# In a graph kernel's four narrow passes, gathers wait for the messages made from a ring's old rows, and the message writers wait for TensorE's sums

## The reference

```python
# first network, per layer
msg = h[src] * edge_weight[:, None]
h_neigh = segment_sum(msg, dst, num_segments=n) * inv_deg
h = h @ W_self[l].T + h_neigh @ W_neigh[l].T + b_neigh[l]
# second network, per layer
a = a_mu + jnp.exp(a_ls) * eps          # eps: one row of 64 for each edge
h = h * norm_out
m = h[src] * a
agg = segment_sum(m, dst, num_segments=n)
h = agg * norm_in @ W + b
```

## Time and profile before

| | |
|---|---|
| median of 3 runs | 11618.99 us (11612.03 to 11624.92) |
| the profiled execution | 11611.31 us, its span 11609.5 us |
| PE busy | 7401.4 us (64%) |
| DVE busy | 7264.5 us (63%) |
| POOL busy | 5339.7 us (46%) |
| ACT busy | 2333.6 us (20%) |
| gathers of the narrow passes (L526 from the node table) | 2496 of them, 2373.6 us busy, 1832.8 us idle ahead of them |

### The profile page before, as it was taken

The page is one execution under the profiler, slowest core; times in us unless marked ns, Lnnn a source line. Parts: engine busy times, 40 slices in busy tenths (PEclk is TensorE's granted clock), DMA queues, the critical chain, the costliest instruction groups (busy, mean ns, idle before and its releaser), DMA issues. The chain is left out here.

```text
span 11609.5 us, 162406 instructions
## 1 busy us (share of the span) xinstructions
PE 7401.4 (64%) x38309; PEld 5189.5 (45%) x38310; DVE 7264.5 (63%) x10358; ACT 2333.6 (20%) x8740; POOL 5339.7 (46%) x5631
## 2 busy tenths in 40 slices
PE   5887788677767765555558465654845555755557
PEld 4665566555555542333257233334732223623336
DVE  6665333455555555777799576778955556755558
ACT  1222444200000001111179111115910000000000
POOL 4555556455555534666400365650015554055650
PEclk8888888788878876777655666775567776966778
DMA  3333444344444436777569576764933333433333
GB/s 82 88 87 82 111 115 116 92 113 112 113 101 114 114 83 208 234 235 234 169 269 397 177 234 230 234 213 193 415 123 75 77 76 66 121 73 76 77 73 103
DMA packets 847434, 1713.98 MB, mean 148 GB/s; under 512 B 384448, under 2 KB 470131, under 8 KB 793063
## 3 DMA queue, kind: packets, MB, share of 16 engines
q1 hardware_dynamic: 462202, 1136.31, 28.3%
q0 software_dynamic: 206896, 411.57, 16.1%
q10 hardware_dynamic: 178256, 165.14, 4.2%
HBM read 1260.10 MB, written 452.33 MB: 148 GB/s over the span
## 5 line engine op out<-in xcount | busy, mean ns | idle before, releaser
L526 POOL DMA_INDIRECT gathered_rows<-node_table,index x2496 | 2373.6, 951 | 1832.8 <-issue 657.6
L691 PE MATMUL ps_G<-table_parts,low_onehots 125*128 125x320 bf16 x15600 | 2719.4, 337 | 278.6 <-issue 187.6
L546 PE MATMUL ps_sum<-messages,onehots 128*125 128x65 f32 (+3 forms) x13312 | 2110.0, 320 | 970.0 <-issue 629.7
L546 PEld LDWEIGHTS ps_sum<-messages,onehots 128*125 128x125 f32 x13312 | 2005.8, 235 | 1095.9 <-issue 1088.0
L526 POOL DMA_INDIRECT gathered_rows<-xl_table,index x1664 | 1572.5, 945 | 1972.1 <-issue 997.0
L526 POOL DMA_INDIRECT gathered_rows<-rel_table,index x1456 | 1383.9, 950 | 2113.6 <-ACT index L516 1177.7
L1507 PE MATMUL ps_Z<-xr,onehots_wide 125*128 x3328 | 1521.4, 616 | 1157.4 <-issue 638.9
L691 PEld LDWEIGHTS ps_G<-table_parts,low_onehots 125*128 125x128 bf16 x15600 | 1677.0, 110 | 1174.2 <-issue 270.3
L721 DVE TENSOR_TENSOR rows_by_feature<-ps_G,fifth_onehots 128x320 f32<-128x320 f32 x1040 | 507.3, 488 | 2475.9 <-remote 1853.1
L1507 PEld LDWEIGHTS ps_Z<-xr,onehots_wide 125*128 125x128 f32 x3328 | 809.3, 260 | 1869.1 <-issue 1776.8
L1555 DVE TENSOR_TENSOR z<-gathered_rows,ps_Z 128x650 f32<-128x650 f32 x832 | 671.1, 827 | 807.5 <-issue 430.3
(11 more groups left out here) (327 smaller groups left out, 7020.4 us busy)
## 6 DMA issues: line engine op xcount, KB each, us to landing
stash_a<-gathered_rows SPq DMA_DIRECT2D x208, 1300.0 KB
kept_rows<-stash_a SPq DMA_DIRECT2D x208, 1300.0 KB
onehots<-onehots_kept SPq DMA_DIRECT2D x520, 500.0 KB
onehots_turned<-onehots_turned SPq DMA_DIRECT2D x416, 250.0 KB
stash_r<-gathered_rows ACTq DMA_DIRECT2D x208, 272.0 KB
kept_rows<-stash_r SPq DMA_DIRECT2D x208, 272.0 KB
low_rows<-low_rows SPq DMA_DIRECT2D x416, 125.0 KB
onehots_kept<-onehots ACTq DMA_DIRECT2D x104, 500.0 KB
```

What stands on the lines that cost most here:

```text
L526: pool.indirect_dma_start(G[:, HALF * k + q, 0:width], None, table, bass.IndirectOffsetOnAxis(IDX[:, k, q:q + 1], 0)).then_inc(gathered[k] ...
L546: return nc.tensor.matmul(ps_sum[0:BN, bass.ds(at, width)], S[:, j, :], M, start=False, stop=True, skip_group_check=True)
L691: last = nc.tensor.matmul(ps_G[:, (fetch * k + g) % 2, 0:D * FIVE], OT[0:BN, k, g, a, :], HP[:, part, a, :, :].rearrange("p f b -> p (f b) ...
```

## The change

A new wait `rows_read(engine, i, k)` is passed when the messages of group n - 4 are made. In the two kinds of narrow pass POOL's gathers, and DVE's pick of fetched rows, wait in it in place of `chunks_free`: the old rows of `G` may be overwritten once the messages have been made from them. The makers of the messages, ACT in `weighted_sums` and DVE in `attribute_sums`, get a wait in `chunks_free` ahead of writing `M`, which the sums of group n - 4 read. The credit of `messages_made` is raised from 2 to 4, so that the first four groups pass `rows_read` at once; all its readers count through `at`, which takes the credit in. SP's and ACT's waits ahead of the loads of one-hots and attributes, and DVE's wait ahead of the one-hots of the first pass, stay on `chunk_done`.

```diff
-        msg_made = Counted("messages_made", 2)
+        msg_made = Counted("messages_made", K)
...
+        def rows_read(engine, i, k):
+
+            engine.wait_ge(msg_made.sem, msg_made.at(K * (i - 1) + k + 1))
...
             if rows_of is None:
-                chunks_free(dve, i, k)
+                rows_read(dve, i, k)
...
-                        gather_loop(pool, G, D, node_table, IDX, chunks_free, HALF - FETCH)
+                        gather_loop(pool, G, D, node_table, IDX, rows_read, HALF - FETCH)
...
                                 act.wait_ge(row_picked.sem, row_picked.at(FETCH * (n + 1)))
+                                chunks_free(act, i, k)
                                 for q in range(HALF):
...
-                        gather_loop(pool, G, D, node_table, IDX, chunks_free, HALF - FETCH)
+                        gather_loop(pool, G, D, node_table, IDX, rows_read, HALF - FETCH)
...
                                 dve.wait_ge(row_picked.sem, row_picked.at(FETCH * (n + 1)))
+                                chunks_free(dve, i, k)
                                 v.tensor_tensor(M[:, group_of(k), :], G[:, group_of(k), :], ps_A[:, :, :], ALU.mult).then_inc(msg_made.sem, 1)
```

## The result

The changed kernel takes **12,267.1 us** (median of 4 runs, 12,244.6 to 12,290.1) beside 11,620.7 us for the kernel before on the same chip: a ratio of 1.0559, 95% interval 1.0546 to 1.0571. It is 646 us slower; 12,350 had been predicted, with 11,680 to 12,620 as the range. The profiled execution has a span of 12,265.1 us, against 11,609.5.

What follows compares the result with a forecast made beforehand. POOL's gathers were taken to hold PE's late posts, so an earlier gate lengthens runs and moves the stall: 146 + 151 + 162 + 269 = 728 us on 11,611.3 gives 12,339, plus 7.7 for the median, 12,350 us; range 11,680 to 12,620.

Steps and rivals of the forecast that it cites:

- about 4 us: Narrow passes: PE's posts later than this into a run of gathers are held until 1.4 us after the run.
- the 2.4: DVE or ACT gets PE's held post 2.4 us after the end of a run of two groups.
- First weighted pass: Two groups in 14.7 + 9.8 = 24.5 us, 12.25 a group against 9.66: +269 us.
- the cycle: Per kind of narrow pass: two groups of gathers, 14.7 us, then a POOL wait of 7.4 to 9.8 us for messages.
- Attribute passes: Two groups in 14.7 + 7.5 = 22.2 us, 11.1 a group against 9.70 and 9.65: +146 and +151 us.
- Second weighted pass: Two groups in 14.7 + 7.4 = 22.1 us, 11.05 a group against 9.49: +162 us.
- a second group follows at once: Second weighted pass: transposes 2.3 us into the run pass, ACT's second messages end at E + 13.7, so runs are pairs.
- the second half of the rule: Narrow passes: a held PE post comes out only after the run of gathers, 1.4 us behind it.
- Faster: Rival, narrow passes: longer runs do not hold posts, PE sets some 8.3 us a group; 549 us less, 11,070; chance 0.16.
- Slower still: Rival, narrow passes: runs of three or more groups, sums begun late; 728 + 416 us, 12,760; chance 0.08.
- Mild: Rival, narrow passes: POOL's lead pays itself back, pairs cost 9.8 us a group as now; +74 us, 11,690; chance 0.16.
- the four terms: The worked additions of the four narrow passes, 146 + 151 + 162 + 269 = 728 us.

Runs made afterwards that it cites:

- `PAD = 900`: Changed kernel plus a POOL fill of 900 numbers before each narrow-pass group; 10,252.5 us, 1.0568, repeated 10,253.5 us, 1.0565, both on chips of 9,702 us.
- the pause kernel: Changed kernel plus a POOL fill of 1600 numbers, waited for, ahead of each narrow-pass group; 11,505.6 us, ratio 0.9904 to the kernel before.
- the kernel made for this: Changed kernel with one gather of six and five POOL fills per narrow-pass group; 9,399.8 us, 0.9689, repeated 9,400.9 us, 0.9688, on chips of 9,702 us.
- the kernel with pairs: Kernel before, with POOL waiting only ahead of even groups, for the sums of both, so 12 gathers go in one run; 12,522.5 us, 1.0784.
- the short pause: Changed kernel plus a POOL fill of 300 numbers before each narrow-pass group; 10,048.8 us, 1.0357 (9,702 us chip); 12,091.3 us, 1.0415 (11,610 us kind).
- three gathers a group: Changed kernel with three gathers of six in each narrow-pass group, the other rows left out; 9,235.8 us, 0.9520, on a chip of 9,702 us.

## Why the prediction was right

**What costs.** The step that the prediction rests on, that PE's posts late in a run of gathers are held until 1.4 us after it, 2.4 after a run of two, is borne out by edits from three sides: longer runs without any lead cost more than the change (1.0784), a break long enough takes the loss away and 105 us more (0.9904), and one that is too short leaves most of it (1.0415).

The traces bear out the boundary of "about 4 us" as a rough one. Of PE's banks for which DVE stood idle in the kernel before, 23 of the 210 that ended less than 4 us into a run of gathers came over 0.5 us late, 17 of them among the 38 between 3 and 4 us, and 74 of the 80 that ended between 4 and 7.2 us; in the kernel with `PAD = 900`, on the faster chip, none of 328 did.

In the changed kernel DVE's first pick comes 2.3 to 2.5 us (medians by pass) after a run of two; the 2.4 was read off. Neither DVE's pick nor the makers' waits had a part (1.0004).

**First weighted pass:** 12.25 us a group expected, 12.16 found (1264.3 us), +260 for +269. Every step of the cycle was there: pairs throughout, 9.83 us between them.

**Attribute passes:** 11.1 expected, 10.89 and 10.79 found, +124 and +119 for +146 and +151. The cycle's wait was over-sized and its pattern too regular. After pairs POOL waited 6.8 and 7.0 us where 7.5 had been worked out, and only 39 and 38 runs were pairs; 21 and 23 were single, followed by 4.5 and 3.9 us. A single group with 4.5 takes 11.7 us and one with 3.9 11.1, so it is the pairs, at (14.7 + 6.8) / 2 = 10.75, that make the pass cheaper.

**Second weighted pass:** 11.05 expected, 10.88 found, +145 for +162, but the step "a second group follows at once" failed. Only 17 runs were pairs, followed by 8.0 us; 65 groups stand alone, with waits of 3.46 us in the mean, from 1.0 to 7.1. The prediction let the transposes pass, because they end 2.3 us into the run. In the changed kernel 61 transposes end 2 to 4 us into a run, and 43 of them reach an idle ACT more than 0.5 us late (2.1 us in the mean of the 61). So the boundary was drawn too sharply from the earlier trace rows: earlier posts can be late too. They also break the second half of the rule, since 33 of the 43 reach ACT while the run is still on. Two groups that act as one run across a short break do not explain them all: behind waits of 6 us and more, 27 of 33 transposes that end in a group's first 4 us are late as well. Why is open. That the price hardly moves is in part luck: what was added up as pairs at 11.05 us a group is in the main single groups at 7.2 + 3.46 = 10.7.

**Rivals.** Faster: needed fewer than 4 groups in 10 with a held post; refuted on this chip. Slower still: its mechanism exists, sums drawn out over 10.2 us in the rows from 1606.22, but its price of +416 us did not come on top and the runs stayed at two. That the banks behind those sums would have been held to the run's end anyway may be why; no run shows it. Mild: pairs at 9.8 us, not found. The 80 us by which the sum was too high (728 for the windows' 648) are the four terms above: 9, 17, 22 and 32, all on the same side, so that no error hides another between the passes.

The Trainium skill (SBUF — State Buffer, Who interferes with whom) has a DMA never contend with a compute engine, and PE never wait on anyone. It says so of the ports to SBUF, and no row here shows a port. Read as widely as the prediction read it, that gathers leave PE alone, it does not fit the chip with 11,610 us (transposes 9.9 us late, records of sums 0.7 us and more apart), while the rows of the chip with 9,702 us (0.04 us) agree with it.

**What stays open.** Whether POOL's issuing or the transfers of its gathers hold PE: in the pause kernel the post came out 1.43 us after the last gather with POOL filling, and 1.4 us after it in the earlier trace rows with POOL idle, so filling seems not to matter; but the fill ended within 0.02 us of the post, and the kernel made for this ran where nothing is held.

The end of the transfers alone does not decide it either. The gathers' last packet ends 1.2 us after the last gather (the median) both behind runs of one group and behind runs of two; the transposes' posts follow at 1.5 us in the first case (the kernel before) and at 2.5 us in the second (the kernel with pairs). And on the faster chip, with `PAD = 900`, packets go on to 2.1 us after the last gather, while the posts come 0.9 us ahead of its end.

All times come from executions whose span and clock were recorded; whether PE is held when nothing is recorded, no run here can say.

The change itself was not run on a chip of 9,702 us. There its effect can only be estimated: taking 416 breaks away from the 10,062.7 us of the short pause leaves passes of (3,490.5 - 4 x 103 x 0.85) / 4 = 785 us, and the kernel before must have about the same, since 9,700 less the rest of that kernel (10,062.7 - 3,490.5 = 6,572) is 3,128, or 782 a pass. That is 104 groups of 7.5 us without a wait, so an earlier gate would have nothing to remove. The best version depends on the chip: the pause of 1600 wins 0.96% where the kernel before takes 11,610 us and, to judge by the shorter ones, loses over 5.7% where it takes 9,702.

## What to carry to other kernels

Removing a wait that looks like the bound can remove the only gap in which something else gets through: before crediting an earlier gate, ask what happens to the others' posts while the freed engine runs on without a break, and compare single runs with double ones in the trace of before. If a pair of runs costs more than two single ones, more lead makes it worse, and a deliberate break may be worth more than the lead. Look at the kernel before on more than one chip before tuning against such an effect.

## What the runs showed of the hardware

- Chips differ by more than any change here: the kernel before takes 11,610 to 11,621 us in three sets of runs and 9,702 to 9,703 us in two. In the passes studied the difference is 4,003 us against some 3,128 (the estimate above), and it goes with the held posts: on the slower ones the posts of the transposes over 5 us into a run came out 1.5 us after it (in the pause kernel 2.3 us late in the mean of 76, 2.85 at most), on the faster ones 0.04 to 0.12 us after PE's end. The rest of the kernel, which nothing here changes, is shorter there too, 6,564 to 6,572 us for 7,606. What sets the chips apart no run shows.
- Late in a run PE not only posts late, it issues slowly: records of sums that take 0.12 us apiece in the earlier trace rows (1.95 / 16) start 0.7, 1.4 or 2.1 us apart in the stretch read above, from 8.6 us into a run of two groups on.
- The granted clock in the narrow passes was 0.83 to 0.86 before, 0.77 to 0.80 after, 0.98 to 0.99 with three gathers a group on the other kind of chip; on the chips of 11,610 us it is lowest, 0.74 to 0.78, in the kernel with pairs, whose passes are the longest.
